# Second attention projection: reciprocal root moved from GpSimd to ScalarE and VectorE, with VectorE's steps in another order

## What is computed

```python
x = x + attn_a(layernorm(x))   # causal, unit norm, rotary
x = x + ffn(layernorm(x))      # 64 experts, 4 per row, and 2 shared ones
x = x + attn_b(layernorm(x))   # not causal, bias on the output
x = x + ffn(layernorm(x))      # the same weights again
```

## Time and profile before

| What | Value |
|---|---|
| Median of three runs | 1237.13 us (1236.69 to 1238.62) |
| The profiled execution | 1233.89 us |
| Its span, first to last instruction | 1232.1 us |
| Mean granted TensorE clock | 0.862 of full speed |
| Busy: PE, PEld, DVE | 924.1, 705.7, 701.2 us |
| Busy: ACT, POOL | 448.6, 505.2 us |
| The second projection | about 574 to 700 us of the span |

### The profile page before, as it was taken

One profiled execution on the slowest core, in us unless ns is written; L12 is line 12 of the kernel. 1 busy time (PEld: TensorE's weight loads), 2 busy tenths in 40 slices (PEclk: granted clock), 3 DMA queues, 4 the chain that ended last, 5 costly groups with the idle time before them and its releaser, 6 DMA issues.

```text
span 1232.1 us, 23970 instructions
## 1 busy us (share of the span) xinstructions
PE 924.1 (75%) x7700; PEld 705.7 (57%) x7700; DVE 701.2 (57%) x1839; ACT 448.6 (36%) x955; POOL 505.2 (41%) x566
## 2 busy tenths in 40 slices
PE   3985899976399988895557599996759997889000
PEld 2764677746288766683445345545648876777000
DVE  4777777735945433353467689943975543445333
ACT  2552555542011244452233168871201144455000
POOL 3000422216477422233785343214377632232676
PEclk9997999986699998998677679997679998999555
DMA  6284899949842489873387367705242359995343
GB/s 228 56 171 81 167 218 217 258 103 243 185 141 102 140 254 267 256 242 119 100 190 193 64 98 108 104 1 144 61 138 102 123 181 238 274 273 186 120 131 115
DMA packets 159010, 196.99 MB, mean 160 GB/s; under 512 B 17328, under 2 KB 137648, under 8 KB 155824
## 3 DMA queue, kind: packets, MB, share of 16 engines
q1 hardware_dynamic: 99744, 94.56, 35.4%
q0 software_dynamic: 22848, 68.18, 17.2%
q10 hardware_dynamic: 36304, 32.84, 9.1%
HBM read 132.86 MB, written 90.18 MB: 181 GB/s over the span
## 4 chain that ended last, share of the span: by engine, by line
PE 24%; DVE 8%; DMA 6%; POOL 5%; issue 3%; SPq 2%; ACT 2%; ACTq 2%; DVEq 0%; POOLq 0%
PE ps L783 4%; POOL big L522 4%; PE ps L823 4%; PE ps L633 3%; DMA yd<-tmp 3%; PE ps L602 3%; DMA big<-yd,slot 2%; PE ps L618 2%; PE ps L794 2%; PE ps L835 2%; PE ps L806 1%; ACTq L310 1%; PE ps L710 1%; SPq L342 1%; SPq L350 1%
## 5 line engine op out<-in xcount | busy, mean ns | idle before, releaser
L853 ACT ACTIVATE tmp<-ps 128x256 f32<-128x256 f32 (+1 forms) x328 | 145.3, 472 | 125.5 <-PE ps L806 32.0
L940 ACT ACTIVATE tmp<-ps 128x384 f32<-128x384 f32 (+1 forms) x256 | 135.7, 544 | 72.4 <-PE ps L621 46.5
L480 POOL DMA_INDIRECT xd<-big,slot x128 | 126.4, 987 | 83.3 <-DVE slot L1334 44.9
L522 POOL DMA_INDIRECT big<-yd,slot x128 | 131.1, 1024 | 42.0 <-issue 25.5
L448 POOL COPY arena<-negmax 24x2048 bf16<-24x2048 bf16 x32 | 60.6, 1893 | 175.7 <-ACT negmax L853 175.7
L602 PE MATMUL ps<-arena 96*128 96x256 bf16 (+1 forms) x512 | 105.8, 278 | 13.2 <-DVEq L285 10.6
L618 PE MATMUL ps<-arena 120*128 120x256 bf16 (+1 forms) x512 | 100.8, 264 | 0.9 <-POOL arena L448 0.3
L1391 DVE SCALAR_TENSOR_TENSOR tmp<-tmp,ps 128x128 f32<-128x128 f32 x128 | 36.8, 287 | 104.0 <-ACT tmp L1009 103.3
L1078 DVE SCALAR_TENSOR_TENSOR X<-big,comb,X 128x256 f32<-128x256 f32 (+1 forms) x128 | 57.9, 481 | 66.7 <-DMA big<-yd,slot 66.7
L1401 DVE COPY tmp<-ps 128x256 f32<-128x256 f32 x128 | 53.7, 424 | 68.6 <-PE ps L835 37.5
L1184 DVE TENSOR_REDUCE tmp<-ps 128x2 f32<-128x512 f32 x128 | 81.6, 683 | 7.8 <-PE ps L602 7.8
(11 more groups left out here) (168 smaller groups left out, 1917.4 us busy)
## 6 DMA issues: line engine op xcount, KB each, us to landing
big<-xd POOLq DMA_DIRECT2D x128, 256.0 KB, 4.7
arena<-parts SPq DMA_DIRECT2D x192, 128.0 KB, 5.6
xd<-zero SPq DMA_DIRECT2D x8, 2048.0 KB, 14.1
spill<-in_we SPq DMA_DIRECT2D x128, 128.0 KB, 3.2
yd<-tmp POOLq DMA_DIRECT2D x64, 256.0 KB, 3.2
yd<-tmp ACTq DMA_DIRECT2D x64, 256.0 KB, 3.5
parts<-arena SPq DMA_DIRECT2D x128, 96.0 KB
arena<-in_we SPq DMA_DIRECT2D x8, 1024.0 KB, 9.2
```

Of the source, the lines that this page charges most:

```text
L480: pool.indirect_dma_start(xd[:, :], bass.IndirectOffsetOnAxis(ap=slot[:, i, k:k + 1], axis=0), xn_all[:, i, :], None).then_inc(scattered.s ...
L522: pool.indirect_dma_start(gring[n % GRING], None, yd[:, :], bass.IndirectOffsetOnAxis(ap=slot[:, b * TB + m % TB, m // TB:m // TB + 1], ax ...
L853: return act.activation(dst, src, ACT.Copy)
L940: act.activation(prob[h % 8][:, 0:n], ps[2 + h % 2][:, 0:n], ACT.Exp).then_inc(exp_ready.sem, 1)
```

## The change

In the second projection GpSimd no longer takes the root. ScalarE takes the square root of bve into a new tile bsd at the head of its step, ahead of the copy to xt; the second part of the batch before also moves ahead of that copy. VectorE takes the reciprocal of bsd. VectorE's order within a step becomes: combine(b), statistics and bve (b), rest (b-1), reciprocal and xn (b), bias (b), last part (b-1). PE, ACT and DVE run this stage with all nine steps written out, by `straight` or a plain loop in the program that builds the kernel. GpSimd's two casts now wait for the last addition of the stage in place of the last root. The first projection keeps its work and order; its function loses the branches of run 1. Cut to its core:

```diff
+def straight(items, depth, unroll, step):
+
+    for s in range(items + depth):
+        step(s, s % unroll, [0 <= s - d < items for d in range(depth + 1)])
+
...
+        bsd = sb("bsd", [P, TB])
...
                 else:
-                    pool.wait_ge(brstd_ready.sem, B)
+                    pool.wait_ge(*g_used(0, NT * K))
                 mark_heads(0)
                 mark_heads(1)
                 pool.wait_ge(*hot_ready(r, 2))
...
-                def batch_rstd(b):
-                    pool.wait_ge(bve_ready.sem, b + 1)
-                    pool.tensor_tensor(brstd[:, :], bve[:, :], mhalf[:, 0:TB], ALU.pow).then_inc(brstd_ready.sem, 1)
                 for b in range(B):
                     for m in range(TB * K):
                         n = b * TB * K + m
@@ -522,10 +526,6 @@
                         pool.indirect_dma_start(gring[n % GRING], None, yd[:, :],
                                                 bass.IndirectOffsetOnAxis(ap=slot[:, b * TB + m % TB, m // TB:m // TB + 1], axis=0)
                                                 ).then_inc(g_in[n % GRING].sem, 16)
-                    if r == 0 and b:
-                        batch_rstd(b - 1)
-                if r == 0:
-                    batch_rstd(B - 1)
 
...
-                pipeline(pe, B, 2 - r, 2, project_step)
+                if r == 0:
+                    pipeline(pe, B, 2, 2, project_step)
+                else:
+                    straight(B, 1, 2, project_step)
                 barrier(pe, "pe")
...
                 def project_step(s, i, has):
                     last = 2 - r
+                    if has[0] and r == 1:
+                        act.wait_ge(bve_ready.sem, s + 1)
+                        act.activation(bsd[:, :], bve[:, :], ACT.Sqrt).then_inc(bsd_ready.sem, 1)
+                    if has[last] and r == 1:
+                        second_part(s - 1, 1 - i)
                     if has[0]:
                         act.wait_ge(*xT_done(r, s + 1))
                         act.wait_ge(*v_done(r, s))
@@ -877,8 +885,6 @@
                     if has[last] and r == 0:
                         act.wait_ge(qf_ready.sem, n + 1)
                         first_part(n, k, qf[k])
-                    if has[last] and r == 1:
-                        second_part(n, k)
                     for side in range(2):
                         if has[0]:
...
-                pipeline(act, B, 2 - r, 2, project_step)
+                if r == 0:
+                    pipeline(act, B, 2, 2, project_step)
+                else:
+                    straight(B, 1, 2, project_step)
                 barrier(act, "act")
...
                 dve.wait_ge(baggr_done.sem, (b + 1) * TB)
                 settle()
+                dve.wait_ge(bsd_ready.sem, b)
                 dve.tensor_scalar(bve[:, :], bmv[:, :, 1], EPS_LN, None, ALU.add).then_inc(bve_ready.sem, 1)
+
+            def batch_normalise(b):
+
+                dve.wait_ge(*xT_done(1, b))
+                dve.wait_ge(bsd_ready.sem, b + 1)
+                dve.reciprocal(brstd[:, :], bsd[:, :]).then_inc(brstd_ready.sem, 1)
                 dve.wait_ge(brstd_ready.sem, b + 1)
                 settle()
                 for tt in range(TB):
-                    dve.tensor_scalar(xn[:, tt, :], X[:, bass.ds(b * TB + tt, 1), :].rearrange("p a d -> p (a d)"),
-                                      bmv[:, tt, 0:1], brstd[:, tt:tt + 1], ALU.subtract, ALU.mult).then_inc(xn_ready.sem, 1)
+                    dve.tensor_scalar(xn[:, tt, :], X[:, b * TB + tt, :], bmv[:, tt, 0:1], brstd[:, tt:tt + 1],
+                                      ALU.subtract, ALU.mult).then_inc(xn_ready.sem, 1)
+
+            def split_rest(b):
+
+                dve.wait_ge(*p1_ready(1, b + 1))
+                dve.wait_ge(*p2_ready(1, b))
+                dve.wait_ge(*p3_ready(1, b))
+                dve.tensor_tensor(res, qr[b % 2], pt[b % 2][:, 0, :], ALU.subtract).then_inc(res_ready.sem, 1)
+
+            def split_last(b):
+
+                dve.wait_ge(*p2_ready(1, b + 1))
+                dve.tensor_tensor(pt[b % 2][:, 2, :], res, pt[b % 2][:, 1, :], ALU.subtract).then_inc(p3_ready.sem, 1)
+
+            def add_bias(b):
+
+                xb = X[:, b * TB:b * TB + TB, :]
+                dve.wait_ge(*xn_ready(1, (b + 1) * TB))
+                dve.tensor_tensor(xb, xb, bproj[:, :].rearrange("p (a d) -> p a d", a=1).broadcast_to([P, TB, D]),
+                                  ALU.add).then_inc(bias_added.sem, 1)
 
...
                 def project_step(s, i, has):
-                    last = 2 - r
-                    if has[0] and r == 1:
-                        combine(0, s, i)
                     if has[0]:
                         dve.wait_ge(*xT_done(r, s))
-                        if r == 0:
-                            wait_rstd(r, 1, s)
-                            normalise(s, xn_ready)
-                        else:
-                            batch_norm(s)
-                    if r == 0 and has[2]:
+                        wait_rstd(r, 1, s)
+                        normalise(s, xn_ready)
+                    if has[2]:
...
-                    if has[last]:
-                        n = s - last
-                        src, part = (qf[i], pt[i]) if r == 0 else (qr[1 - i], pt[1 - i])
+                    if has[2]:
+                        n = s - 2
+                        src, part = qf[i], pt[i]
                         dve.wait_ge(*p1_ready(r, n + 1))
                         dve.wait_ge(*p2_ready(r, n))
                         dve.wait_ge(*p3_ready(r, n))
                         dve.tensor_tensor(res, src, part[:, 0, :], ALU.subtract).then_inc(res_ready.sem, 1)
-                        if r == 1:
-
-                            xb = X[:, bass.ds((s - 1) * TB, TB), :]
-                            dve.wait_ge(*xn_ready(r, s * 2))
-                            dve.tensor_tensor(xb, xb, bproj[:, :].rearrange("p (a d) -> p a d", a=1).broadcast_to([P, TB, D]),
-                                              ALU.add).then_inc(bias_added.sem, 1)
                         dve.wait_ge(*p2_ready(r, n + 1))
                         dve.tensor_tensor(part[:, 2, :], res, part[:, 1, :], ALU.subtract).then_inc(p3_ready.sem, 1)
-                    if has[1] and r == 0:
...
-                pipeline(dve, B, 2 - r, 2, project_step)
+                if r == 0:
+                    pipeline(dve, B, 2, 2, project_step)
+                else:
+                    for b in range(B + 1):
+                        if b < B:
+                            combine(0, b, b % 2)
+                            batch_norm(b)
+                        if b >= 1:
+                            split_rest(b - 1)
+                        if b < B:
+                            batch_normalise(b)
+                            add_bias(b)
+                        if b >= 1:
+                            split_last(b - 1)
                 barrier(dve, "dve")
```

More of the change, by code:

```diff
@@ L255, in build @@
         bstat_done, baggr_done = signal("bstat_done"), signal("baggr_done")
-        bve_ready, brstd_ready, stored = signal("bve_ready"), signal("brstd_ready"), signal("stored")
+        bve_ready, bsd_ready, brstd_ready, stored = signal("bve_ready"), signal("bsd_ready"), signal("brstd_ready"), signal("stored")
         FIRST = ("ident", "rotm", "headsum", "headsel", "cs", "gain", "wqk0", "wv0")
@@ L1127, in project_step @@
                         dve.tensor_tensor(roped, roped, rt2, ALU.add).then_inc(qf_ready.sem, 1)
-                    if has[1] and r == 0:
+                    if has[1]:
                         dve.wait_ge(nrm_ready.sem, s)
```

## The result

The changed kernel took 1232.10 us (median of 20 runs, 1220.34 to 1243.80), the kernel before 1237.89 us in 20 runs beside it (1227.78 to 1245.37). The ratio is 0.9934, 95% interval 0.9905 to 0.9963: faster by 0.4 to 0.95%. That ratio leaves out the runs over 1.5% above the fastest of their kernel, five of the changed one and none of the kernel before; with all 20 of each the medians give 0.9953. The forecast was 1230.8 us, faster. But single executions of one kernel differ by up to 1.4 and 1.9%, and in the experiments the kernel before took 1237 us at some times and 1357 us at others, with the other sign for the change: read the rest with both in mind.

What follows compares the result with a forecast made beforehand. Bound: second projection, its normalised tiles paced by GpSimd's gathers and power. Earlier tiles, cut back by b2's store and the casts, save 6.3 us: execution 1233.89 to 1227.6, plus 3.2 to the median, 1230.8 us; range 1223.5 to 1235.

Steps and rivals of the forecast that it cites:

- GpSimd's power stood too late: Second projection: b0's power stands behind b1's eight gathers, so xn of b0 starts 6.7 us late.
- The table load at nothing: One load at the stage's first Sqrt, one when exponentials return, both on idle ScalarE: 0 us, 2.6 if uncovered.
- The drain: Skill's 2.66 us per change of table set including drain: two switches 5.3 us if uncovered, saving down to 1.0.
- rival 5: Second projection: table loaded at each Sqrt and back, two loads a batch, 1245 us; chance 0.03.
- Loop over the tensor engine, 11.7 us: From xn to next xn: delay to ScalarE's first part 9.0, copy 1.06, rest 1.22, reciprocal and gaps 0.4 us.
- ScalarE's Sqrt cost nothing behind the value copy: Sqrt of b behind b-1's value copy is hidden beside the 1.22 us rest: 0 us; uncovered 0.3 us a batch.
- SP's loads and stores cap the gain: SP's work from the 24 loads on moves up only 9.5 to 10 us; b4's first part waits for b2's store.
- The rest of b6 beside a cast waits: Stage's tail: b6's rest waits for GpSimd's casts until 678.1; xn of b7 ends at 680.1 to 680.5, against 686.4.
- The sum, 6.3 us: Whole kernel 6.3 us less, through xn of b7 ending earlier with the same work after it; time 1230.8 us.
- The chance of slower, 0.09: Stores hold up first parts of b5 and b6, 1243 us (0.06), or table loads at each Sqrt, 1245 us (0.03).
- Written-out steps at nothing: Second projection's loops of three iterations written out: 0 us, plus or minus 1 us for code and register work.

Runs made afterwards that it cites:

- Root only: Kernel before with ScalarE's Sqrt and VectorE's reciprocal in place of GpSimd's power, old order and loops kept: ratio 1.0101 where the kernel before takes 1357 us.
- power early: Kernel before with GpSimd's power moved from behind the next batch's eight gathers to behind its fourth: ratio 1.0041 where the kernel before takes 1357 us.
- Late loads: Changed kernel with the 24 stack loads moved behind the stores of b4 and b5: ratio 1.0005 where the kernel before takes 1357 us.
- kernel of three edits: Changed kernel with stack loads later, casts after b6's last part, one-column Sqrt at ScalarE's stage head: 1217.91 us, 0.9846; 0.9977 where the kernel before takes 1357 us.
- kernels with a pause: GpSimd holds b2's first gather until b0's values are copied: changed kernel 1.0006; with late loads, late casts, early Sqrt 0.9922; loads one store later 0.9841.
- order only: Changed kernel with the root back on GpSimd behind the next batch's gathers, new order and written-out steps kept: ratio 1.0037 where the kernel before takes 1357 us.

## Why the prediction was right, and where it was wrong

- **GpSimd's power stood too late: right.** Root only and power early show it on b0. That the periods after it fall by the same cause isn't shown apart from the new order. From the first gather, xn of b0 came at 16.0 us where the working had 14.9.
- **The table load at nothing: wrong.** I put it where ScalarE is idle. It waited with the Sqrt for the variance: 1.28 us on the path (586.42). With a Sqrt ahead of it, xn of b0 starts at 14.7 us. The drain that the Trainium skill counts in "ScalarE: Activation LUTs", section "What ACT_TABLE_LOAD costs", is not seen here: from the load's start to the end of the Sqrt it is 1.50 us. Nor is it at a load of the first projection, at 30.11 us in the same trace, right behind a copy that ends at 30.09 and ahead of an instruction that starts at 31.41. The eight Sqrts took one load, and the one for the exponentials (703.06) ended while ScalarE had to wait for TensorE anyway, so rival 5 is out.
- **Loop over the tensor engine, 11.7 us: right on the whole.** 12.1, 10.8, 10.7 us, and up to 12.5 with the loads away. ScalarE's Sqrt cost nothing behind the value copy.
- **SP's loads and stores cap the gain: right in mechanism, too small in size.** The loads began 619.28 - 572.33 = 47.0 us after the first gather (forecast 46). But b2's store took 20.9 us from its first issue (631.72 to 652.60), where I had carried over 15.8. It ended 80.3 us after the first gather in place of 75.1, and the first part of b4, which waited 3.73 us for it, set xn of b5: that is the 3.9 us by which b5 missed its forecast. b4's additions also ended late, at 63.6 us and not 60.6, but without the wait for the store the first part of b4 would have started at 648.9, so b5 lost nothing more by them. Late loads took the wait away.
- **The rest of b6 beside a cast waits: right.** It took 3.40 us in place of 1.22 and ended 1.1 us after the casts. The variance of b7 was held as well (2.25 us). From the end of the additions (672.02) to the end of xn it was 9.3 us; the working had 9.4. The Trainium skill, "SBUF — State Buffer", section "Who interferes with whom", holds here. In the kernel of three edits, whose casts start only at 682.62, the same rest takes 1.23 us (678.50).
- **The sum, 6.3 us: 3.8 us in the stage of the profiled pair**, 5.8 us between the medians of 20 runs. The term that was sized too small is b2's store, 15.8 us for 20.9. That the span came out to the tenth is luck: 2.5 of its 6.3 us lie outside the stage. I had also said that this measurement tells 0.2% from no change; with 20 runs of each, the interval is 0.3% to either side.
- **The slow condition: not foreseen.** The chance of slower, 0.09, rested on stores and table loads. Where the kernel before takes 1357 us, the change costs 0.4 to 1.2%, and what its profile has for it is neither, but one wait of ScalarE beside 32 gathers without a break. The power that was removed had been a break after 16 and after 24 of them; that its going brings the wait is not shown.
- **Written-out steps at nothing:** not tested in the fast condition. In the slow one a pair of profiles has 10 us from b1 on for them, the times show no difference.

## What to carry to other kernels

A small instruction behind a long run of issues on the same engine can cost the run, not its own time: look at where it stands before moving it elsewhere. When a wait is taken away, ask which bulk transfers stand ahead of the next small one in the same queue; here 24 loads were issued 75 us before the stage that needs them. The periods beside them fell by 10.4 us in the kernel with the loads moved, against 3.8 us for the change, though in the fast condition the loads were only moved together with the other two edits. And put the first use of a function table where its operand's wait can't hold it.

## What the runs showed that I had not expected

The same program took 1237 us at some times and 1357 us at others, and a chip with the number 7 stands in both. In the slow condition engines wait up to 44.0 us for something that the trace can't place on the core, mostly beside runs of 8 to 64 indirect transfers that GpSimd issues 0.3 us apart. In the fast condition the same runs stand beside no such wait. What is waited for is not shown by any run. One guess would be the program's code, but in the changed kernel the profile's two instruction queues move nothing between 655 and 680 us, where the 18.25 us wait runs and ends. Whether a pause of GpSimd lifts it is open, since the kernels with a pause ran in the fast condition. That power early and order only, where GpSimd breaks off for 0.9 us once a batch, have 6.6 and 9.4 us as their longest wait ahead of a copy of q or k, and the kernels without a break 17.2 to 18.9, speaks for it, no more.
